# Score tiles further ahead of the softmax pass, and another order of DMAs and events, in a hand-scheduled attention and FP4 feed-forward block

## Reference

```python
c_kv = x @ W_dkv.T                       # 64 latents
q = (x @ W_dq.T @ W_uq.T).reshape(B, T, 16, 8)
q_lat = einsum('bqhd,hdl->bhql', q, k_eff)
attn = softmax(where(causal, einsum('bhql,bkl->bhqk', q_lat, c_kv) / sqrt(8), -inf))
y = einsum('bhql,hld->bqhd', einsum('bhqk,bkl->bhql', attn, c_kv), v_eff)
x = layernorm(x + y)                     # y as (B, T, 128)
gate, up = fp4_linear(x, w_gate), fp4_linear(x, w_up)    # 352 wide
x = layernorm(x + fp4_linear(silu(gate) * up, w_down))
# fp4_linear: each block of 16 is divided by max|.|/6, rounded to 0, .5, 1, 1.5, 2, 3, 4, 6, multiplied back
```

## Time and profile before

| | us |
|---|---|
| median of 3 runs | 665.78 |
| the profiled execution | 664.24 |
| its span | 662.3 |
| busy: TensorE / VectorE / ScalarE / GpSimd | 531.8 / 513.0 / 440.0 / 335.3 |
| first t tile's exponential starts | 47.9 |
| last t tile's exponential ends | 599.8 |

### The profile page before, as it was taken

How to read it: one execution, slowest core, us unless ns; L and a number is a source line. 1 busy time by engine, 2 the same in 40 slices (tenths; PEclk the granted TensorE clock), 3 DMA queues, 4 the chain that set the end, 5 groups by cost and what they waited for, 6 DMA issues and landing times.

```text
span 662.3 us, 15225 instructions
## 1 busy us (share of the span) xinstructions
PE 531.8 (80%) x5866; PEld 246.0 (37%) x5866; DVE 513.0 (77%) x867; ACT 440.0 (66%) x663; POOL 335.3 (51%) x518
## 2 busy tenths in 40 slices
PE   6276789988798989989899899988978998695352
PEld 3133244333343434434344335334433353232232
DVE  1497689888878868788898778797979784638795
ACT  3322557777588888786688888885869788665230
POOL 5630013110456776655666866565676666617353
PEclk9656799999989999999999999999999999788586
DMA  3469004822120085020400571020200000000000
GB/s 84 105 161 221 27 2 88 203 48 59 35 72 19 12 182 146 1 58 18 122 18 3 113 181 46 4 72 26 66 3 20 2 3 3 0 17 17 0 17 16
DMA packets 33624, 37.97 MB, mean 57 GB/s; under 512 B 5344, under 2 KB 19616, under 8 KB 33552
## 3 DMA queue, kind: packets, MB, share of 16 engines
q1 hardware_dynamic: 33552, 37.00, 23.3%
HBM read 19.64 MB, written 16.78 MB: 55 GB/s over the span
## 4 chain that ended last, share of the span: by engine, by line
PE 34%; DVE 26%; issue 16%; POOL 14%; ACT 8%; DMA 1%; SPq 0%; POOLq 0%; DVEq 0%; ACTq 0%
DVE top L1044 13%; PE yt_ps L752 10%; PE ring L714 5%; PE ring L731 5%; PE misc L666 3%; ACT probs L904 3%; PE misc L684 3%; PE ring L698 2%; DVE hc L1165 1%; POOL hx L1466 1%; POOL hx L1464 1%; DVE top L1041 1%; PE misc L651 1%; POOL eg L1524 1%; POOL k_part L1406 1%
## 5 line engine op out<-in xcount | busy, mean ns | idle before, releaser
L1044 DVE TENSOR_REDUCE top<-ring 128x2 f32<-128x1024 f32 (+1 forms) x320 | 311.4, 1004 | 63.8 <-PE ring L698 32.6
L904 ACT ACTIVATE probs<-ring 128x1024 f32<-128x1024 f32 x288 | 291.5, 1025 | 75.0 <-PE ring L731 38.4
L752 PE MATMUL yt_ps<-probs,v_op 128*32 128x512 f32 (+3 forms) x1536 | 161.5, 509 | 2.6 <-ACT probs L904 2.6
L714 PE MATMUL ring<-k_op,q_op 56*128 56x512 f16 (+3 forms) x768 | 122.2, 343 | 29.1 <-DMA q_op<-scratch_q 13.1
L731 PE MATMUL ring<-q_op,k_op 59*128 59x512 bf16 (+3 forms) x768 | 120.5, 337 | 30.1 <-DVE top L1044 20.4
L714 PEld LDWEIGHTS ring<-k_op,q_op 56*128 56x128 bf16 x768 | 37.4, 94 | 136.8 <-issue 81.2
L731 PEld LDWEIGHTS ring<-q_op,k_op 59*128 59x128 f16 x768 | 37.2, 93 | 97.3 <-issue 47.7
L1519 POOL TENSOR_TENSOR r<-r,yq 128x128 f32<-128x128 f32 x32 | 14.9, 466 | 104.9 <-DVE yq L1087 104.9
L698 PE MATMUL ring<-ident,mask_s 64*128 64x64 bf16 x1024 | 57.1, 193 | 0.0
L698 PEld LDWEIGHTS ring<-ident,mask_s 64*128 64x128 bf16 x1024 | 45.8, 98 | 16.8 <-issue 2.4
L698 PEld LDWEIGHTS ring<-ident,mask_t 64*128 64x128 bf16 x1024 | 44.8, 96 | 15.2 <-issue 1.3
(11 more groups left out here) (197 smaller groups left out, 798.1 us busy)
## 6 DMA issues: line engine op xcount, KB each, us to landing
q_op<-scratch_q SPq DMA_DIRECT2D x30, 224.0 KB
k_op<-scratch_k SPq DMA_DIRECT2D x30, 224.0 KB
scratch_k<-k_part SPq DMA_DIRECT2D x32, 192.0 KB, 3.3
scratch_q<-q_part SPq DMA_DIRECT2D x32, 128.0 KB, 3.1
scratch_q<-q_part SPq DMA_DIRECT2D x16, 192.0 KB, 3.3
xp<-in_L_attn_x_dram SPq DMA_DIRECT2D x4, 512.0 KB, 4.3
r<-in_L_attn_x_dram SPq DMA_DIRECT2D x8, 256.0 KB, 3.0
out_dram<-z SPq DMA_DIRECT2D x6, 256.0 KB, 2.2
```

Source lines behind the costliest of these rows:

```text
L714: last = nc.tensor.matmul(ring[slot][:, e, at:at + n], q_op[lo:lo + ROWS, pair, i * P:(i + 1) * P], k_op[lo:lo + ROWS, pair, kc * CHUNK:kc ...
L752: last = nc.tensor.matmul(yt_ps[32 * q:32 * (q + 1), lo:CHUNK], v_op[:, j, 4 * a + q, :], probs[:, place[tile] % P_RING, q % 2, at:at + CH ...
L904: nc.scalar.activation(probs[:, n % P_RING, :, :], ring[slot("t", b * BODY + n)][:, :, :], ACT.Exp, scale=SCALE).then_inc(t_exp.sem, 1)
L1044: last = nc.vector.tensor_reduce(top[:, kc, :, p, i], ring[slot][:, :, at:at + w], AX.X, ALU.max)
```

## The change

`LEAD` goes from 6 to 12, so 30 s tiles stand ahead instead of 24. `EARLY` gets 60 entries in place of 31 and reaches the new lead at step 58: against before, one more tile stands ahead at step 5 (and at most of the steps from there to 35), three at step 36, five at step 47, six from step 57 on. In the last batch the s tiles end at step 41 instead of 47. `MT` goes from 2 to 3. For the first batch, SyncE sends the maxima's rows of the second unit ahead of the operands of quads 2 and 3 and of the fourth quad's `scratch_out`. Nearly all tables of steps are new; most entries move by one step or none.

```diff
-LEAD = 6
+LEAD = 12
-    W_STEP = [3, 5, 6, 6, 10, 11, 12, 15, 16, 17, 17, 18]
+    W_STEP = [3, 5, 5, 6, 10, 11, 12, 15, 16, 17, 18, 18]
-    EARLY = [11, 13, 14, 18, 20, 22, 23, 25, 26, 27, 28, 30, ... 50, 51, 53, 54]
+    EARLY = [11, 13, 14, 18, 20, 22, 24, 26, 26, 28, 29, 31, ... 60, 61, 64, 65, ... 74, 77, 77, 78, 78, 80, 82, ... 88, 89]
-    YN, MT, OUT = [4, 2], 2, [0, 0]
+    YN, MT, OUT = [4, 2], 3, [0, 0]
...
-        "xt": [7, 9], "k": [15, 16], "krest": [18, 21], "q": [21, 23], "v": [19, 25],
+        "xt": [6, 9], "k": [13, 16], "krest": [18, 21], "q": [21, 22], "v": [18, 24],
...
-        "zstat0": [86, 87, 101, 105], "zmean": [86, 87, 114, 116], "zrstd": [88, 90, 115, 116], "znorm": [90, 92, 115, 116],
+        "zstat0": [86, 86, 101, 105], "zmean": [86, 87, 114, 117], "zrstd": [88, 88, 117, 117], "znorm": [91, 91, 117, 119],
...
             scratch_out(0, 2)
-            scratch_out(0, 3)
-            operands_in(0, 2)
-            operands_in(0, 3)
             residual_in(0, 0)
-            residual_in(0, 1)
             next_tokens_in(0)
             max_rows_in(0, 1)
+            operands_in(0, 2)
+            scratch_out(0, 3)
+            operands_in(0, 3)
+            residual_in(0, 1)
```

More of the change, by code:

```diff
@@ L179, in slot @@
         return PLACE[kind, n] % 3
-    YN, MT, OUT = [4, 2], 2, [0, 0]
+    YN, MT, OUT = [4, 2], 3, [0, 0]
     FFN = {
[L186 to L190, removed]
+        "gate": [4, 8, 17, 24, 30, 35, 41, 48], "up": [6, 14, 22, 25, 32, 37, 42, 50], "clamp": [4, 8, 20, 27, 32, 36, 45, 49],
+        "ln": [6, 14, 22, 28, 33, 37, 45, 51], "sig": [6, 14, 22, 29, 33, 37, 45, 51], "h": [7, 14, 23, 29, 33, 39, 50, 52],
+        "amax": [11, 15, 24, 30, 34, 42, 50, 52], "hwide": [11, 15, 24, 32, 37, 42, 50, 52], "hinv": [11, 16, 25, 32, 39, 42, 50, 53],
+        "hdiv": [11, 17, 26, 32, 39, 42, 50, 53], "hexp": [12, 19, 26, 33, 40, 43, 51, 54], "hmagic": [13, 23, 27, 36, 42, 44, 52, 55],
+        "hround": [13, 23, 27, 37, 42, 45, 57, 58], "ht": [19, 26, 31, 43, 49, 51, 60, 63],
     }
     NEXT = {
-        "xt": [7, 9], "k": [15, 16], "krest": [18, 21], "q": [21, 23], "v": [19, 25],
+        "xt": [6, 9], "k": [13, 16], "krest": [18, 21], "q": [21, 22], "v": [18, 24],
     }
@@ L204, in build @@
     }
     TAIL_FFN = {
-        "gate": [64, 65, 72, 72, 83, 83, 87, 91], "up": [66, 70, 73, 77, 85, 85, 87, 93], "clamp": [64, 66, 72, 72, 83, 83, 88, 93],
-        "ln": [65, 68, 73, 75, 84, 86, 88, 93], "sig": [66, 68, 73, 75, 84, 86, 88, 93], "h": [68, 70, 74, 77, 85, 86, 92, 95],
-        "amax": [68, 70, 75, 77, 85, 86, 93, 95], "hwide": [68, 70, 75, 77, 85, 86, 93, 95], "hinv": [69, 71, 75, 77, 85, 87, 93, 95],
-        "hdiv": [69, 71, 75, 78, 85, 90, 93, 95], "hexp": [69, 73, 76, 78, 85, 92, 93, 98], "hmagic": [69, 73, 76, 78, 85, 92, 93, 98],
@@ L210, in build @@
-        "hround": [69, 76, 78, 78, 88, 92, 98, 100], "ht": [74, 78, 79, 79, 89, 97, 100, 102],
+        "gate": [64, 65, 71, 72, 83, 83, 87, 93], "up": [66, 70, 73, 77, 85, 86, 87, 92], "clamp": [64, 65, 72, 72, 83, 83, 87, 93],
+        "ln": [65, 67, 73, 76, 85, 85, 89, 94], "sig": [65, 68, 73, 76, 85, 86, 89, 94], "h": [66, 70, 74, 78, 85, 86, 92, 95],
+        "amax": [69, 70, 74, 79, 85, 86, 92, 95], "hwide": [69, 70, 76, 79, 85, 86, 93, 95], "hinv": [69, 70, 76, 79, 85, 87, 93, 95],
+        "hdiv": [69, 70, 76, 79, 85, 88, 93, 95], "hexp": [69, 71, 77, 79, 85, 90, 93, 95], "hmagic": [69, 73, 78, 79, 85, 91, 93, 95],
@@ L211, in build @@
+        "hround": [69, 76, 78, 79, 85, 91, 98, 99], "ht": [74, 78, 78, 79, 88, 96, 100, 101],
     }
     TAIL_LAST = {
-        "x1t": [60, 63, 79, 81], "down": [85, 86, 98, 103],
+        "x1t": [61, 67, 79, 83], "down": [84, 86, 100, 103],
     }
     TAIL_NORM = {
-        "lnstat0": [52, 54, 76, 76], "lnmean": [54, 54, 76, 76], "lnrstd": [54, 54, 76, 76], "lnnorm": [54, 54, 79, 79], "xamax": [54, 54, 79, 79],
-        "xinv": [54, 54, 81, 81], "xdiv": [55, 56, 81, 81], "xexp": [58, 59, 81, 81], "xmagic": [59, 60, 81, 81], "xround": [59, 62, 81, 82],
+        "lnstat0": [52, 54, 77, 77], "lnmean": [54, 54, 77, 77], "lnrstd": [54, 55, 77, 77], "lnnorm": [55, 55, 79, 79], "xamax": [55, 55, 79, 79],
```

9 lines of the change are left out of this document (5 added, 4 removed).

## The result

| | before | after |
|---|---|---|
| median, us | 665.65 (665.11 to 666.02) | 669.16 (668.85 to 670.01) |
| the profiled execution, us | 664.24 | 670.01 |
| its span, us | 662.3 | 667.4 |
| busy: TensorE / VectorE | 531.8 / 513.0 | 537.3 / 513.9 |

The account below looks back on a forecast made before the run. No engine bounds the whole kernel; TensorE all but bounds a middle batch. Terms -2.5 + 4.6 - 3.0 - 0.7 - 0.8 = -2.4 us against the median of 665.78 gave 663.4 us, 8-in-10 range 660.0 to 668.3.

Parts of the forecast that it names:

- the stall at t tile 5: First batch: the second unit's rows arrive sooner with fewer transfers in front, a gain of 2.5 us, between nothing and 5.2.
- The last two norms: Kernel's end: with both aggregations first, most of one wait for GpSimd's root goes, a gain of 1.1 us.
- The lead in the last batch: Steps 42 to 47: six s tiles gone, ScalarE next to bound, a return of 3.0 us, between 0.5 and 3.9.
- the lead in the first batch: Steps 36 to 57: five more tiles, 40% of VectorE's idle time filled, a cost of 4.6 us, between 2.4 and 6.1.
- the end: Behind the last exponential: norms gain 1.1 us, another value-matmul group loses 0.3, together 0.8 gained; bounds 2 gained, 1 lost.
- The new tables shift pieces by a step; I can't price each: Three batches: together with `MT` a gain of 0.7 us; bound 1.3 us a batch either way, 4 us over three.
- In the middle batches the lead moves no work ...: nothing.: Middle batches: the lead changes only which s tile stands beside which feed-forward piece, costing nothing.
- `MT`: Transposition of the maxima: one more step ends TensorE's wait for GpSimd's parts, 0.7 us a middle stretch, a third taken.
- The costly lead: Rival, chance 0.22: steps 36 to 57 cost 6.1 us, the last batch returns 0.5; sum +2.1, 667.9 us.
- The rows: Rival, chance 0.14: at t tile 5 the rows come as late as before; sum +0.1 us, 665.9, no change.
- the middle batches went against the gain: Rival, chance 0.13: new tables take waits from TensorE, each middle batch gains 1.3 us; sum -5.7, 660.1 us.
- the clock: Rival, chance 0.09: the last batch's thinner stretch begins earlier and partly runs at the lower clock; about +2.5, 665.9 us.

Follow-up runs that it names:

- e1: The kernel before with SyncE's new queue order alone (second unit's rows ahead of the operands of quads 2 and 3): 661.74 us, ratio 0.992.
- e2: The kernel before with the lead of 30 alone (`LEAD` 12 and a longer `EARLY`), all tables of steps old: 690.56 us, ratio 1.0362.
- e4: The kernel before with the four new `TAIL_` tables alone: 661.6 us, ratio 0.9931.
- e3: The kernel before with the new middle tables alone (`FFN`, `NEXT`, `LAST`, `NORM`, `NORM2`): 675.99 us, ratio 1.0144.
- e5: The kernel before with the new `NEXT` table alone: 673.26 us, ratio 1.0127.
- e9: The kernel before with one number of `NEXT` changed, the second q projection at step 22 in place of 23: 669.56 us, ratio 1.004.
- e13: The kernel before with one number of `NEXT` changed, the first k projection at step 13 in place of 15: 669.56 us, ratio 1.0041.
- e14: The kernel before with the v projections of `NEXT` at steps 18 and 24 in place of 19 and 25: 669.89 us, ratio 1.0044.
- e8: The changed kernel with the old `NEXT` table: 667.15 us, ratio 1.0021 against the kernel before.
- e11: The changed kernel with all five middle tables of before: 681.25 us, ratio 1.0228 against the kernel before.
- e16: The kernel before with SyncE's new order, the new tail tables, `MT` 3 and the new `W_STEP`: 663.81 us, ratio 0.9963.
- e17: The changed kernel with `MT` 2 in place of 3: 675.89 us, ratio 1.016 against the kernel before.
- e12: The changed kernel with the first batch's order of scores (`EARLY`) of before up to step 30: 671.37 us, ratio 1.0061 against the kernel before.
- the square: Four kernels with new queue order, tail tables, `MT` 3, `W_STEP`: lead 24, old/new middle tables 663.8/680.0 us; lead 30, 681.3/669.2 us.

## Why the prediction was wrong

**Right, with the size:** the stall at t tile 5 (2.5 us forecast, 2.9 by t tile 5 and 2.4 by t tile 9), shown to be SyncE's order by e1. The last two norms: 1.1 forecast, 1.16 measured. The lead in the last batch: 3.0 forecast, and steps 258 to 264, which were to take 11.1 us, took 11.7, 2.3 less than before (in e2, with the lead alone, 1.8 less); ScalarE was busy 10.07 us of them, near the 10.2 that the floor was taken from.

**Right in size, in part by luck:** the lead in the first batch, 4.6 forecast and 4.1 measured in steps 36 to 60. The working had five tiles there and 40% of VectorE's idle time filled. VectorE's maxima take only 4.0 us more there (32.8 against 28.8), some three tiles, since the order has three tiles more ahead already at step 36; and nothing was filled: VectorE is busy 4.2 us longer and its idle time stays at 4.4 us (4.5 before). The two errors go against each other.

**Right in sign, too small:** the end, 0.8 forecast and 2.6 measured. The group of value matmuls was set against the norms' gain, and nothing was priced of the pieces ahead of the norms; e4 shows that the tail tables give 3.2 us there.

**Wrong, the step that failed:** "The new tables shift pieces by a step; I can't price each", put at a third of 0.7 us a batch, a gain of 0.7 in all, and bounded by 1.3 us a batch either way. The middle batches lost 3.3 and 2.8 us. In the kernel before, e3 shows the tables doing this much (3.5 each), e5 that `NEXT` is enough for it (3.7 and 3.3), and e9, e13 and e14 that its q, k and v each have a part. The profile of after shows the longest of the new waits among six jobs in a row on the one buffer `misc`, and in the second middle batch 2.9 us more of waits on it. That the tables are all of it in after is not shown, and the runs speak against it: taking `NEXT` back (e8) leaves 141.0 and 141.7 us, and taking all five tables back (e11) makes 146.8 and 145.5. Beside the lead the new tables spare time. The bound was wrong as well: "a tenth of TensorE's idle 13.4 us" was taken from the waits that were there, but a moved job makes new ones. A sign of it was in the trace before: TensorE already waited for that buffer at these steps, 0.4 us behind `yq` and 0.3 behind `gu`.

**Wrong, a term that was missing:** t tiles 9 to 36, 4.3 us. The prediction took one of the six new tiles as free, since maximum 23 falls into the stall. It does, but by step 18 the same number of tiles stands ahead as before, and the sixth is done behind it after all: from t tile 9 to 36 VectorE's maxima take 1.3 us more. e11, which has after's order of scores and the old middle tables, takes 0.9 us more than before in steps 24 to 30 and 1.1 in steps 30 to 36. Another part is `NEXT`: e5 takes 2.0 us more in steps 18 to 24 and gives 1.2 of them back in the next six. In after there is also a stretch at the lower clock there (0.73 granted in 107.27 to 119.72, 1.00 before): TensorE is busy 3.1 us longer from t tile 9 to 36 and idle 1.2 longer. e11, at 1.00 all through these steps, takes 2.7 us more than before. `MT` is another candidate: together with `W_STEP` it brings 4.4 us here (e16), but taking it back in after makes 56.7 us of the 55.1 (e17). How it splits stays open; by e12 it isn't the order of the scores at the start.

**Wrong, an argument:** "In the middle batches the lead moves no work ...: nothing." In e2 the lead alone makes each of them 7 us longer. So which s tile stands beside which piece of feed-forward is worth several microseconds a batch. In after it does not show by itself, as the new tables go with the lead.

**Wrong, `MT`:** it was counted as a gain from one wait of 0.7 us a batch. That wait stayed (0.8 us), and `MT` with `W_STEP` costs 8.8 us without the lead and the new middle tables (e16), while its absence costs 6.7 with them (e17).

**The rivals.** The kernel came out slower, but by none of the four as priced. The costly lead was to lose 6.1 us in steps 36 to 57 and to return 0.5; it lost 4.1 and returned 2.3, though its mechanism, no idle time filled, is what the rows show, and from t tile 24 to 60 e11 loses 6.2. The rows were not late; the middle batches went against the gain; and in the last batch the clock was granted at 0.89 from t tile 264 on, no lower than the 0.85 of before. The lower clock cost time elsewhere, from t tile 24 to 30 and in the first middle batch, where no rival had it. No rival had the tables of the middle batches as a loss.

**What stays open:** why the lead and the middle tables, each worse alone by 16 to 17 us in the square, spare 28 together. The runs show that it is so, and that waits and the lower clock each carry about half of it, not which meetings of tiles and jobs it is.

## What to carry to other kernels

Where the order is written out by hand and many jobs go through one buffer, a table that shifts them by a step is not a small edit that averages out: write down, for the densest steps, the jobs on that buffer in order and who empties each, and price the new neighbours. Take a change of several tables apart and run the parts: two of these (the queue order and the tail tables), which act at different places, gave 4.8 and 4.9 us alone and 10.8 together, while those that act on the same steps (the lead, the middle tables, `MT`) did not add up at all. And if one part of a tuned order is changed, the others are tuned to the old one; neither "each part is harmless" nor "each part hurts" tells what all of them do.
